# A two-pass Strassen FFN kernel: the second half of W is prepared inside the steps of the first pass, kept in DRAM, and loaded back slice by slice

## The chip, the cores and the metric

The kernel runs on one core of one Trainium2 chip. The metric is device time in microseconds from one launch to its end, less is better. The core has a matrix engine (TensorE, PE in the profile), a vector engine (VectorE, DVE), a scalar engine (ScalarE, ACT), GpSimd (POOL), a queue engine that here only issues DMAs (SyncE, SP) and 16 DMA engines. The on-chip memories are SBUF (128 partitions) and PSUM (8 banks of 128 x 512 float32).

## The reference

```python
x = x + _L0_ffn_ref(_L0_cond_ref(x, itok_B_0_30, L0_cond_weights), W_base, b_base, W_gate, A, B)
# _L0_cond_ref: x [32,128,2048], w = weights[subjects] [32,128,128]
return jnp.einsum('bct,bcd->bdt', x, w)
# _L0_ffn_ref: OUT = DIM = 2048, E = 8 experts of rank R = 16, TOP_K = 2
result = jnp.einsum('bnd,od->bno', x, W_base) + b_base
logits = jnp.einsum('bnd,ed->bne', x, W_gate)
probs = softmax(logits); top_p, top_i = top_k(probs, 2); top_p = top_p / sum(top_p)
route_w = sum(one_hot(top_i, E) * top_p[..., None])
hw = jnp.einsum('bnd,erd->bner', x, A) * route_w[..., None]
return result + jnp.einsum('bner,eor->bno', hw, B) * SCALING
```

So each of 32 blocks of 128 tokens is multiplied by a small matrix of its own, and the result (128 x 2048) by W (2048 x 2048), with a bias, a routed low-rank term and the input added.

## The kernel before

**Tiling.** The contraction is cut in two: the first pass (steps n = 0 to 15) works with columns 0 to 1023 of W, the second (steps 16 to 31) with columns 1024 to 2047. A step takes two of the 32 blocks. The product of the block pair with half of W is done by a Strassen-Winograd scheme: seven products (`NPROD = 7`) of sub-blocks, each for two halves `s` of the outputs, so 14 products a step. Every operand is split into an upper and a lower float16 part, and a product is 4 chunks x 3 matmuls of 128 x 512 (`three`, L1121 to L1123). The first pass writes its sums to DRAM (`part_scratch`), the second loads them, adds its own and stores to the output.

**What W has to become.** `TT` holds the seven prepared right-hand operands (B11, B22, B21 and four sums T1 to T4), upper and lower parts, for both `s`. There is room in SBUF for one half of W. It is prepared by units `g` (eight to a half): load rows (`load_rows`), sum of magnitudes per row (`sum_rows`, L582, ACT), powers of two as scales (`w_scales`, DVE), turn on PE with a scaled diagonal (`w_quad`, L1150) and spread of the inverse scale (`spread`, L1132), upper parts on ACT (`upper`, L603 and L610), sums and lower parts on DVE (`w_sums_and_lower`), last lower parts on POOL (`w_lower`, L450). Units 0 to 7 are done at the start, around step 0. Units 8 to 15 are done between steps 15 and 16, when nothing reads `TT` any more: at the end of step 15 PE waits for the last tiles and then turns all eight (L1367 to L1374), and before step 16 it waits for all of `w_lo`, `w_sum_lo` and `w_inv` (L1341 to L1344).

**One step of the loop.** No scheduler is at work: each engine runs its own list in the order in which it is written, with semaphores between them. PE: product q0 of s = 0, `make_features` (bank_h, 48 matmuls of 136 columns), `transpose_maxima` (L1207), products q1 and q2, `spread_maxima` (L1211), then the other products with four `cond` groups for step n+1 (bank_c) between them. `cond(n+1, U_A11)` stands after product q5 of s = 0 and waits for `xp_lo`, the lower parts of the scaled x. The chain to it is: product q2, DVE `finish(n, 0, C11)` (L823, L827), DVE `scale_x` (L782 to L786), ACT `split_x_hi` (L529, L530), DVE `split_x_lo` (L791, L793). POOL adds the bias (L456) and the step's results (L475) to the 128 x 512 tiles of `x_res`. ACT copies finished banks (`copy_p`, L571; `copy_a`, L537) and makes upper parts of the left operands (`s_upper`, L556). SP stores and loads tiles (`store_tile`, `load_tile`), x and the small weights (`load_x`). The buffer `x_parts` (XP) holds the split x of the next step from `split_x_hi` until the last `cond` of the step.

## Time and profile before

| | us |
|---|---|
| median of 3 runs | 1634.38 (1634.27 to 1634.62) |
| the profiled execution | 1634.34 |
| its span, first to last instruction | 1632.6 |
| PE busy | 1536.8 (94%) |
| DVE busy | 1300.2 (80%) |
| ACT busy | 596.5 (37%) |
| POOL busy | 631.9 (39%) |
| DMA, mean | 124 GB/s, 39.8% of 16 engines |

The profiled execution is within 0.04 us of the median, and lies 1.7 us above its own span. The table is an average over two passes and two stretches of preparation. The page's 40 slices and a table by stretch tell these apart. Since one line of code serves many instructions, groups are read by tile: bank_x, bank_y and bank_z are products, bank_h features, bank_c `cond` and the maxima, bank_d the second pass's deltas.

### The profile page before, as it was taken

Reading aid. Unit: us, or ns where it says so; the run is one execution under the profiler, and the core shown is the slowest. Engines: PE = TensorE matmul, PEld = TensorE weight load, DVE = VectorE, ACT = ScalarE, POOL = GpSimd, SP = SyncE. Lnnn points to the kernel's source line nnn. Section 1 sums busy time; section 2 is a strip of 40 time slices with the busy share of each in tenths; the row PEclk is TensorE's granted clock in tenths of the full one; section 3 lists DMA queues with packets and bytes.
Section 4 is the critical chain, followed back from the end, with each engine's and each line's share of the span. In section 5 each row is a group of like instructions: output and inputs, shape, how many; then the busy total and the mean of one; then the engine's idle time right before and its main releaser. Section 6 shows DMA issues by size and latency. Waiting matters only on the chain.

```text
span 1632.6 us, 25730 instructions
## 1 busy us (share of the span) xinstructions
PE 1536.8 (94%) x9539; PEld 837.8 (51%) x9539; DVE 1300.2 (80%) x2228; ACT 596.5 (37%) x996; POOL 631.9 (39%) x473
## 2 busy tenths in 40 slices
PE   5667999999999999999668999999999999999998
PEld 5444555555555555555464555555555555555553
DVE  6666888888888888888776888888888888888874
ACT  6654333333333333333583323333322333332231
POOL 2534455555555555555453122222212221221222
PEclk8788999999999999999889999999999999999999
DMA  5332444444444444444731344343334434333432
GB/s 198 130 117 82 128 136 136 135 135 134 128 136 136 136 127 133 132 134 125 235 104 39 98 137 136 110 122 121 102 91 136 136 113 121 122 105 88 134 107 71
DMA packets 102911, 201.87 MB, mean 124 GB/s; under 512 B 10874, under 2 KB 24186, under 8 KB 102266
## 3 DMA queue, kind: packets, MB, share of 16 engines
q1 hardware_dynamic: 102786, 200.22, 39.8%
q8 instruction: 76, 1.25, 0.3%
q14 instruction: 49, 0.40, 0.1%
HBM read 128.96 MB, written 71.22 MB: 123 GB/s over the span
## 4 chain that ended last, share of the span: by engine, by line
PE 89%; DVE 5%; ACT 2%; issue 2%; DMA 1%; POOL 1%; POOLq 0%; SPq 0%; DVEq 0%; ACTq 0%
PE bank_x L1121 10%; PE bank_x L1122 10%; PE bank_x L1123 10%; PE bank_y L1123 10%; PE bank_y L1122 10%; PE bank_y L1121 10%; PE bank_z L1121 3%; PE bank_z L1123 3%; PE bank_z L1122 3%; PE bank_h L1122 3%; PE bank_h L1121 3%; PE bank_h L1123 3%; PE bank_c L1121 2%; PE bank_c L1123 2%; PE bank_c L1122 2%
## 5 line engine op out<-in xcount | busy, mean ns | idle before, releaser
L475 POOL TENSOR_TENSOR x_res<-x_res,t_sums 128x512 f32<-128x512 f32 x256 | 350.7, 1372 | 895.6 <-DVE t_sums L827 735.5
L1121 PE MATMUL bank_x<-TT,s_parts 128*128 128x512 f16 x768 | 295.5, 385 | 14.8 <-POOL TT L450 7.5
L1122 PE MATMUL bank_x<-TT,s_parts 128*128 128x512 f16 x768 | 295.0, 384 | 0.0
L1123 PE MATMUL bank_x<-TT,s_parts 128*128 128x512 f16 x768 | 294.6, 384 | 0.0
L1121 PE MATMUL bank_y<-TT,s_parts 128*128 128x512 f16 x768 | 291.2, 379 | 0.0
L1122 PE MATMUL bank_y<-TT,s_parts 128*128 128x512 f16 x768 | 291.1, 379 | 0.0
L1123 PE MATMUL bank_y<-TT,s_parts 128*128 128x512 f16 x768 | 291.1, 379 | 0.0
L571 ACT ACTIVATE p_copies<-bank_x,y_inv 128x512 f32<-128x512 f32 x128 | 87.8, 686 | 492.8 <-PE bank_x L1123 398.7
L827 DVE TENSOR_TENSOR t_sums<-t_sums,inv_w 128x512 f32<-128x512 f32 x256 | 218.6, 854 | 8.8
L800 DVE TENSOR_TENSOR s_parts<-a_full,s_parts 128x512 f16<-128x512 f32 x224 | 208.1, 951 | 7.5 <-ACT s_parts L556 7.5
L456 POOL TENSOR_TENSOR x_res<-x_res,BT 128x512 f32<-128x512 f32 x128 | 197.8, 1545 | 4.8 <-DMA x_res<-in_x_dram 3.3
L556 ACT ACTIVATE s_parts<-a_full 128x512 f16<-128x512 f32 x224 | 137.2, 627 | 117.3 <-DVE a_full L805 49.5
L823 DVE SCALAR_TENSOR_TENSOR t_sums<-bank_y,y_inv,p_copies 128x512 f32<-128x512 f32 x128 | 95.5, 746 | 103.1 <-PE bank_y L1123 102.3
L1121 PEld LDWEIGHTS bank_x<-TT,s_parts 128*128 128x128 f16 x768 | 75.8, 99 | 100.6 <-issue 19.0
L823 DVE SCALAR_TENSOR_TENSOR t_sums<-bank_x,y_inv,p_copies 128x512 f32<-128x512 f32 x128 | 95.4, 745 | 38.3 <-PE bank_x L1123 38.3
L1123 PEld LDWEIGHTS bank_x<-TT,s_parts 128*128 128x128 f16 x768 | 76.0, 99 | 93.3 <-issue 4.6
L1123 PEld LDWEIGHTS bank_y<-TT,s_parts 128*128 128x128 f16 x768 | 75.2, 98 | 90.7 <-issue 0.2
L537 ACT ACTIVATE a_full<-bank_c 128x512 f32<-128x512 f32 x128 | 76.2, 595 | 122.1 <-PE bank_c L1123 122.1
L1122 PEld LDWEIGHTS bank_x<-TT,s_parts 128*128 128x128 f16 x768 | 76.0, 99 | 84.8 <-issue 3.3
L1122 PEld LDWEIGHTS bank_y<-TT,s_parts 128*128 128x128 f16 x768 | 75.2, 98 | 81.7 <-issue 0.3
L1121 PEld LDWEIGHTS bank_y<-TT,s_parts 128*128 128x128 f16 x768 | 75.2, 98 | 81.2 <-issue 0.3
L1121 PE MATMUL bank_c<-w_cond_parts,x_parts 128*128 128x128 f16 x512 | 93.7, 221 | 3.7 <-ACT a_full L537 3.7
(219 smaller groups left out, 2715.6 us busy)
## 6 DMA issues: line engine op xcount, KB each, us to landing
x<-in_x_dram SPq DMA_DIRECT2D x32, 1024.0 KB, 5.7
x_res<-in_x_dram SPq DMA_DIRECT2D x128, 256.0 KB, 3.7
part_scratch<-x_res SPq DMA_DIRECT2D x128, 256.0 KB, 2.9
x_res<-part_scratch SPq DMA_DIRECT2D x128, 256.0 KB, 3.9
out_dram<-x_res SPq DMA_DIRECT2D x128, 256.0 KB, 2.8
x_parts<-in_L_ffn_W_base_dram SPq DMA_DIRECT2D x12, 512.0 KB, 5.3
a_full<-in_L_ffn_W_base_dram SPq DMA_DIRECT2D x12, 512.0 KB, 4.8
w_cond<-in_L_cond_weights_dram SPq DMA_DIRECT2D x64, 64.0 KB, 3.9
```

The lines of the kernel that those rows point to most:

```text
L456: link(nc.gpsimd.tensor_tensor(XR[:, xr_slot(m), :], XR[:, xr_slot(m), :], bias[:, o:o + Q], ALU.add))
L475: nc.gpsimd.tensor_tensor(XR[:, xr_slot(m), :], XR[:, xr_slot(m), :], TM[:, m % 2, :], ALU.add).then_inc(r_added, 1)
L537: nc.scalar.activation(AF[:, u, :], BC[:, :], ACT.Copy, scale=Y_DOWN).then_inc(af_copied, 1)
L556: nc.scalar.activation(SO[:, slot(n, q), 0, :, :], quads(AF[:, af_of[q], :]), ACT.Copy).then_inc(s_hi, 1)
L571: nc.scalar.activation(PC[:, at, :], src[:, :], ACT.Copy, scale=y_inv[:, par, row:row + 1]).then_inc(p_copied, 1)
L800: nc.vector.tensor_tensor(SO[:, slot(n, q), 1, :, :], quads(AF[:, af_of[q], :]), SO[:, slot(n, q), 0, :, :], ALU.subtract).then_inc(s_lo, 1)
L823: nc.vector.scalar_tensor_tensor(out=TM[:, m % 2, :], in0=src[:, :], scalar=y_inv[:, n % 2, c // 2:c // 2 + 1], in1=PC[:, at, :], op0=ALU. ...
L827: nc.vector.tensor_tensor(TM[:, m % 2, :], TM[:, m % 2, :], inv_w[:, o:o + Q], ALU.mult).then_inc(r_ready, 1)
L1121: nc.tensor.matmul(dst, lhs[0], rhs[0], start=start, stop=False, skip_group_check=chained)
L1122: nc.tensor.matmul(dst, lhs[0], rhs[1], start=False, stop=False, skip_group_check=chained)
L1123: return nc.tensor.matmul(dst, lhs[1], rhs[0], start=False, stop=stop, skip_group_check=chained)
```

## The change

The preparation of units 8 to 15 moves into steps 1 to 15 of the first pass, under new numbers g = 0 to 7. A unit is cut into four chunks of 128 columns. `WINDOWS` gives each step two chunks, and step 7 all four of unit 3, so that 15 steps do 32 chunks.

- SP loads the unit's rows into `x_parts` once the last `cond` of the step has read it (`load_rows_ahead`), again for the second window.
- At the end of the step before a unit's first window ACT sums the rows (`sum_rows_ahead`), DVE makes scales (`scales_ahead`), PE spreads them into bank_d (`spread_ahead`); ACT scales the rows in place in front of every window (`scale_rows_ahead`).
- A chunk is turned by four float32 transposes into bank_d (`turn_chunk`), copied by ACT into a half of `a_full` (`copy_chunk`), added up to the four sums by four 128 x 128 operations on POOL (`add_up`), split into an upper part of 128 x 896 by ACT (`upper_chunk`) and a lower part of 128 x 896 by DVE (`lower_chunk`).
- SP stores each part to DRAM (`store_piece`, 896 pieces of 256 bytes, 64 stores). Three buffers take turns; they lie in `late_words`, a region shared with names that the first preparation and the second pass use.
- In step 15 ACT issues 14 loads of 1 MB, one for each q and s, as soon as that slice's last product is done (`load_weights`), and each product of step 16 waits for its own slice (`t_in`). `inv_w` goes through DRAM too. The loads of `FT`, `h_first` and `BT` for the second pass come earlier.
- `SLOTS` goes from 10 to 9, and `copy_p(n, 1, U2_COPY)` comes ahead of the upper part of S3. The whole block between steps 15 and 16 is gone.

The diff, cut to its core, in the order names, SP, POOL, ACT, DVE, PE:

```diff
-SLOTS = 10
+SLOTS = 9
...
+        NPIECE = 3
+        pieces = late_words[:, 0:1344].bitcast(F16).rearrange("p (i q n) -> p i q n", i=NPIECE, q=NPROD)
...
+        WINDOWS = []
+        for g in range(NU):
+            WINDOWS += [(g, (0, 1, 2, 3))] if g == WHOLE else [(g, (0, 1)), (g, (2, 3))]
+        SAVED = (B11, B22, B21, T1, T3, T2, T4)
...
+            def load_rows_ahead(g, chunks):
+                s, r = g // 4, g % 4
+                for i in range(2):
+                    o = s * KH + i * Q + r * P
+                    if chunks[0] == 0:
+                        sp.dma_start(xp_rows[:, i, :], w_base[o:o + P, KH:T]).then_inc(bg_rows[i], 16)
...
+            def store_piece(g, c, part):
+                s, r = g // 4, g % 4
+                sp.wait_ge((bg_hi, bg_lo)[part], n_chunk(g, c))
+                at = piece(g, c, part)
+                sp.dma_start(wt_dram[:, s, :, part, c, r * P:(r + 1) * P].rearrange("q p n -> p q n"), pieces[:, at, :, :]
+                             ).then_inc(bg_out[at], 16)
...
+                g, chunks = window_of(n)
+                if chunks:
+                    if chunks[0] == 0:
+                        store_inv(g)
+                    store_piece(g, chunks[0], 0)
+                    store_piece(g, chunks[0], 1)
+                    store_piece(g, chunks[1], 0)
...
                     store_tile(m)
+                    if len(chunks) == 2 and j == 0:
+                        store_piece(g, chunks[1], 1)
...
-                    if n == NP - 1 and j == 3:
+                    if n < len(WINDOWS) and j == (4 if n == 0 else 3):
+                        sp.wait_ge(cond_done, 4 * (n + 2))
+                        load_rows_ahead(*window_ahead(n))
...
-                    for g in range(NU + 2, 2 * NU):
-                        sp.wait_ge(w_tr, 4 * (g - 1))
-                        load_rows(g)
+                    load_inv(1)
...
+            def add_up(g, c):
+                chunk = full[c % 2].rearrange("p (i n) -> p i n", i=8)
+                pool.wait_ge(bg_copied, n_chunk(g, c))
+                nc.gpsimd.tensor_tensor(chunk[:, 5, :], chunk[:, 2, :], chunk[:, 0, :], ALU.subtract)
+                link(nc.gpsimd.tensor_tensor(chunk[:, 4, :], chunk[:, 0, :], chunk[:, 1, :], ALU.subtract))
+                link(nc.gpsimd.tensor_tensor(chunk[:, 6, :], chunk[:, 2, :], chunk[:, 4, :], ALU.subtract))
...
+                    g, chunks = window_of(n - 1)
+                    if chunks:
+                        act.wait_ge(bg_tr, n_chunk(g, chunks[-1]))
...
+                if chunks and u in (0, 2):
+                    act.wait_ge(bg_lo, n_chunk(g, chunks[-2 + u // 2]))
...
+            def sum_rows_ahead(g):
...
+                for i in range(2):
+                    act.wait_ge(bg_rows[i], 16 * n_window(g, 0))
+                    ins = nc.scalar.activation(late_words[:, 0:KH].bitcast(F16)[:, i * KH:(i + 1) * KH],
+                                               xp_rows[:, i, :], ACT.Abs, accum_out=row_sum[:, 0, i:i + 1])
+                ins.then_inc(bg_sums, 1)
+            def scale_rows_ahead(g, chunks):
+                act.wait_ge(bg_scaled, g + 1)
+                for i in range(2):
+                    act.wait_ge(bg_rows[i], 16 * n_window(g, chunks[0]))
+                    rows = halves(xp_rows[:, i, :], chunks)
+                    ins = nc.scalar.activation(rows, rows, ACT.Copy, scale=row_scale[:, i:i + 1])
+                ins.then_inc(bg_rows_scaled, 1)
...
+            def copy_inv_ahead(g):
+                act.wait_ge(bg_spread, g + 1)
+                if g > 0:
+                    act.wait_ge(bg_inv_out, 16 * g)
+                nc.scalar.copy(inv_piece, BD[:, 0:2 * P]).then_inc(bg_inv, 1)
+            def copy_chunk(g, c):
+                act.wait_ge(bg_tr, n_chunk(g, c))
+                if g == WHOLE and c >= 2:
+                    act.wait_ge(bg_lo, n_chunk(g, c - 2))
+                else:
+                    act.wait_ge(s_lo, NPROD * (n_window(g, c) + 1))
+                nc.scalar.activation(full[c % 2][:, 0:Q], BD[:, :], ACT.Copy).then_inc(bg_copied, 1)
+            def upper_chunk(g, c):
+                act.wait_ge(bg_sum, n_chunk(g, c))
+                at = piece(g, c, 0)
+                if piece_turn(g, c, 0) > 16:
+                    act.wait_ge(bg_out[at], piece_turn(g, c, 0) - 16)
+                nc.scalar.activation(pieces[:, at, :, :], full[c % 2][:, P:8 * P].rearrange("p (q n) -> p q n", q=NPROD),
+                                     ACT.Copy).then_inc(bg_hi, 1)
+            def load_weights(s, q):
+                act.wait_ge(prod_done, n_prod(NP - 1, s, q))
...
+                act.dma_start(TT[:, q, s, :, :, :], wt_dram[SAVED.index(q), s, :, :, :, :]).then_inc(t_in[s][q], 16)
...
+                if chunks and chunks[0] == 0:
+                    copy_inv_ahead(g)
...
+                if chunks:
+                    copy_chunk(g, chunks[0])
+                    copy_chunk(g, chunks[1])
+                    upper_chunk(g, chunks[0])
                 copy_p(n, 0, P5_COPY)
+                if chunks:
+                    upper_chunk(g, chunks[1])
+                if whole:
+                    copy_chunk(g, chunks[2])
                 copy_p(n, 0, U2_COPY)
...
+                if fresh:
+                    for q in range(4):
+                        load_weights(0, q)
...
                     lift_s(n + 1, U_A22, A22)
                     s_upper(n + 1, S4)
+                    copy_p(n, 1, U2_COPY)
                     s_upper(n + 1, S3)
-                    copy_p(n, 1, U2_COPY)
+                    if fresh:
+                        for q in range(5):
+                            load_weights(1, q)
...
+                g, chunks = window_ahead(n)
+                if chunks and chunks[0] == 0:
+                    sum_rows_ahead(g)
+                elif chunks:
+                    scale_rows_ahead(g, chunks)
                 copy_p(n, 1, P4_COPY)
-                if n == NP - 1:
-                    sum_rows(NU)
-                    for g in range(NU, 2 * NU):
-                        if g + 1 < 2 * NU:
-                            sum_rows(g + 1)
-                        w_upper(g)
-                    act.wait_ge(w_sum_lo, 4 * 2 * NU)
+                if chunks and chunks[0] == 0:
+                    scale_rows_ahead(g, chunks)
...
+            def scales_ahead(g):
+                dve.wait_ge(bg_sums, g + 1)
+                power_of_two(row_pow2[:, :], row_sum[:, 0, :], row_clamped[:, :])
+                link(nc.vector.reciprocal(row_rpow2[:, :], row_pow2[:, :]))
+                if g > 0:
+                    dve.wait_ge(bg_rows_scaled, n_window(g, 0) - 1)
+                    dve.wait_ge(bg_spread, g)
+                nc.vector.tensor_scalar(row_scale[:, :], row_rpow2[:, :], TOP_W, None, ALU.mult).then_inc(bg_scaled, 1)
...
+                ins.then_inc(bg_diag, 1)
+            def lower_chunk(g, c):
+                dve.wait_ge(bg_hi, n_chunk(g, c))
+                if n_chunk(g, c) > 1:
+                    dve.wait_ge(bg_lo, n_chunk(g, c) - 1)
+                at = piece(g, c, 1)
+                if piece_turn(g, c, 1) > 16:
+                    dve.wait_ge(bg_out[at], piece_turn(g, c, 1) - 16)
+                nc.vector.tensor_tensor(pieces[:, at, :, :], full[c % 2][:, P:8 * P].rearrange("p (q n) -> p q n", q=NPROD),
+                                        pieces[:, piece(g, c, 0), :, :], ALU.subtract).then_inc(bg_lo, 1)
...
+                if chunks:
+                    lower_chunk(g, chunks[0])
...
                     scale_x(n + 1)
+                if chunks and not whole:
+                    lower_chunk(g, chunks[1])
...
+                if ahead_chunks and ahead_chunks[0] == 0:
+                    scales_ahead(ahead)
...
-                if n == NP - 1:
-                    dve.wait_ge(r_added, 8 * NP)
-                    w_scales(NU)
-                    for g in range(NU, 2 * NU):
-                        if g + 1 < 2 * NU:
-                            w_scales(g + 1)
-                        w_sums_and_lower(g)
...
+                if n == NP:
+                    pe.wait_ge(t_in[s][q], 16)
...
+            def spread_ahead(g):
+                pe.wait_ge(bg_diag, g + 1)
...
+                mm.then_inc(bg_spread, 1)
+            def turn_chunk(g, c):
+                pe.wait_ge(bg_rows_scaled, n_window(g, c))
+                if c == 0:
+                    pe.wait_ge(bg_inv, g + 1)
+                else:
+                    pe.wait_ge(bg_copied, n_chunk(g, c - 1))
+                for i, (block_of, half) in enumerate(((1, 0), (0, 0), (1, 1), (0, 1))):
+                    mm = nc.tensor.transpose(BD[:, i * P:(i + 1) * P],
+                                             xp_rows[:, block_of, half * Q + c * P:half * Q + (c + 1) * P], ident[:, :])
+                mm.then_inc(bg_tr, 1)
...
                 product(n, 0, 0)
+                if chunks:
+                    turn_chunk(g, chunks[0])
                 make_features(n)
                 if more:
                     transpose_maxima(n + 1)
+                if chunks:
+                    turn_chunk(g, chunks[1])
...
-                if n == NP - 1:
-                    pe.wait_ge(p_copied, n_copy(n, 1, P4_COPY))
-                    pe.wait_ge(t_done, n_tile(n, 1, C22))
-                    pe.wait_ge(h_ready, NP)
-                    for g in range(NU, 2 * NU):
-                        pe.wait_ge(stage_in[2 * g % 4], 16 * (g // 2 + 1))
-                        pe.wait_ge(stage_in[(2 * g + 1) % 4], 16 * (g // 2 + 1))
-                        w_quads(g)
+                if ahead_chunks and ahead_chunks[0] == 0:
+                    spread_ahead(ahead)
```

**Order on PE**, in a step of the first pass, at the end of the features (bank_h) and the start of product q1 (bank_y). Before:

```order
2278 L1122 MATMUL bank_h<-FT,s_parts 128x136
2279 L1123 MATMUL bank_h<-FT,s_parts 128x136
2280 L1121 MATMUL bank_h<-FT,s_parts 128x136
2281 L1122 MATMUL bank_h<-FT,s_parts 128x136
2282 L1123 MATMUL bank_h<-FT,s_parts 128x136
2283 L1207 MATMUL bank_c<-ident,amax 4x128
2284 L1121 MATMUL bank_y<-TT,s_parts 128x512
```

After, in the step that begins a unit; here the spread, the end of product q0 with the first turn, and the second turn:

```order
2243 L1471 MATMUL bank_d<-diag_inv,ones 128x128 x2
...
2254 L1358 MATMUL bank_x<-TT,s_parts 128x512
2255 L1359 MATMUL bank_x<-TT,s_parts 128x512
2256 L1481 MATMUL bank_d<-ident,x_parts 128x128 x4
2257 L1357 MATMUL bank_h<-FT,s_parts 128x136
...
2305 L1445 MATMUL bank_c<-ident,amax 4x128
2306 L1481 MATMUL bank_d<-ident,x_parts 128x128 x4
2307 L1357 MATMUL bank_y<-TT,s_parts 128x512
```

Two groups of four float32 transposes stand between product q0 and product q1 of every such step, and a spread in front of q0 where a unit begins.

**Order on DVE**, from the top pair found (`find_top`, L777) to the lower part of x (L791). Before:

```order
280 L777 TENSOR_SCALAR top_diag<-ident,top_pow 4x4
281 L823 SCALAR_TENSOR_TENSOR t_sums<-bank_y,y_inv,p_copies 128x512
282 L827 TENSOR_TENSOR t_sums<-t_sums,inv_w 128x512
283 L782 COPY pow<-bank_c 128x4
284 L783 RECIPROCAL rpow<-pow 128x4
285 L784 TENSOR_SCALAR xw_scale<-rpow 128x4
286 L785 TENSOR_TENSOR x<-x 128x512
287 L786 SCALAR_TENSOR_TENSOR y_inv<-pow 128x2
288 L791 SCALAR_TENSOR_TENSOR x_parts<-x,xw_scale,x_parts 128x1024
```

After:

```order
294 L980 TENSOR_SCALAR top_diag<-ident,top_pow 4x4
295 L1185 TENSOR_TENSOR late_words<-a_full,late_words 128x896
296 L1028 SCALAR_TENSOR_TENSOR t_sums<-bank_y,y_inv,p_copies 128x512
297 L1032 TENSOR_TENSOR t_sums<-t_sums,inv_w 128x512
298 L985 COPY pow<-bank_c 128x4
299 L986 RECIPROCAL rpow<-pow 128x4
300 L987 TENSOR_SCALAR xw_scale<-rpow 128x4
301 L988 TENSOR_TENSOR x<-x 128x512
302 L989 SCALAR_TENSOR_TENSOR y_inv<-pow 128x2
303 L1185 TENSOR_TENSOR late_words<-a_full,late_words 128x896
304 L994 SCALAR_TENSOR_TENSOR x_parts<-x,xw_scale,x_parts 128x1024
```

One lower part stands in front of C11's finish, the other between `scale_x` and `split_x_lo`.

**Order on ACT**, from the end of one step's second half to the upper part of x in the next. Before:

```order
149 L556 ACTIVATE s_parts<-a_full 128x512 x3
150 L571 ACTIVATE p_copies<-bank_x,y_inv 128x512
151 L571 ACTIVATE p_copies<-bank_z,y_inv 128x512
152 L571 ACTIVATE p_copies<-bank_x,y_inv 128x512
153 L571 ACTIVATE p_copies<-bank_y,y_inv 128x512
154 L571 ACTIVATE p_copies<-bank_x,y_inv 128x512
155 L529 ACTIVATE x_parts<-x,xw_scale 128x1024
```

After, where a unit begins:

```order
166 L678 ACTIVATE s_parts<-a_full 128x512
167 L741 ACTIVATE late_words,row_sum<-x_parts 128x1024 x2
168 L693 ACTIVATE p_copies<-bank_z,y_inv 128x512
169 L750 ACTIVATE x_parts<-x_parts,row_scale 128x2x256 x2
170 L757 CAST late_words<-bank_d 128x256
171 L693 ACTIVATE p_copies<-bank_x,y_inv 128x512
172 L765 ACTIVATE a_full<-bank_d 128x512 x2
173 L772 ACTIVATE late_words<-a_full 128x896
174 L693 ACTIVATE p_copies<-bank_y,y_inv 128x512
175 L772 ACTIVATE late_words<-a_full 128x896
176 L693 ACTIVATE p_copies<-bank_x,y_inv 128x512
177 L648 ACTIVATE x_parts<-x,xw_scale 128x1024
```

Nine instructions are woven between the copies that PE and DVE wait for.

## Rows read from the trace of the kernel before

**Rows 1.** The page, 40 slices of the span: PE busy, in tenths.

```profile
PE   5667999999999999999668999999999999999998
```

**Rows 2.** By stretch: us, PE, PEld, DVE, ACT, POOL busy; clock; DMA share; GB/s.

```profile
180.00:780.00 600.00, 600.00 (x3803) 314.78 (x3801) 483.95 (x611) 205.67 (x329) 333.97 (x230) 1.00 0.43 134
780.00:860.00 80.00, 50.57 (x329) 42.54 (x327) 56.56 (x124) 56.47 (x108) 40.87 (x35) 0.85 0.50 162
```

**Rows 3.** Instructions of L1211 (behind product q2), by windows: count, ns, first and last start.

```profile
L1211 PE MATMUL bank_c<-top_diag,ones x1: 173/173/173, 171.4 to 171.4; 4*128 4x4 bf16 x1
...
L1211 PE MATMUL bank_c<-top_diag,ones x1: 172/172/172, 760.8 to 760.8; 4*128 4x4 bf16 x1
...
L1211 PE MATMUL bank_c<-top_diag,ones x1: 173/173/173, 878.5 to 878.5; 4*128 4x4 bf16 x1
```

**Rows 4.** Timeline of PE between steps 15 and 16: start, us, instruction, idle before, releaser.

```profile
800.79 0.37 PE L1132 MATMUL bank_h<-diag_inv,ones 128*128 128x128 bf16 x2 [8.57 <-DVE diag_inv L927]
...
865.68 0.59 PE L1121 MATMUL bank_x<-TT,s_parts 128*128 128x512 f16 x1 [7.45 <-POOL TT L450]
```

**Rows 5.** Timeline of PE: four float32 transposes early on; one, and a product, mid-pass.

```profile
25.09 0.60 PE L1266 MATMUL bank_d<-ident,TT 128*128 128x128 f32 x4
...
460.69 0.27 PE L1207 MATMUL bank_c<-ident,amax 128*4 128x128 f32 x1
460.80 0.38 PE L1121 MATMUL bank_y<-TT,s_parts 128*128 128x512 f16 x1
```

**Rows 6.** Timeline of a step of the first pass: the chain to `cond(n+1, U_A11)`.

```profile
426.92 1.79 POOL L456 TENSOR_TENSOR x_res<-x_res,BT 128x512 f32<-128x512 f32 x1
...
428.99 1.29 DVE L791 SCALAR_TENSOR_TENSOR x_parts<-x,xw_scale,x_parts 128x1024 f16<-128x1024 f32 x1 [0.26 <-ACT w_cond_parts L530]
...
430.20 0.35 DVE L793 SCALAR_TENSOR_TENSOR w_cond_parts<-w_cond,xw_scale,w_cond_parts 128x128 f16<-128x128 f32 x1
...
431.86 0.22 PE L1121 MATMUL bank_c<-w_cond_parts,x_parts 128*128 128x128 f16 x1
...
432.53 0.38 PE L1121 MATMUL bank_x<-TT,s_parts 128*128 128x512 f16 x1
```

**Rows 7.** Timeline of DVE: a lower part of 512 columns, beside POOL's work and without.

```profile
438.67 1.75 DVE L800 TENSOR_TENSOR s_parts<-a_full,s_parts 128x512 f16<-128x512 f32 x1
...
446.49 0.68 DVE L800 TENSOR_TENSOR s_parts<-a_full,s_parts 128x512 f16<-128x512 f32 x1
```

**Rows 8.** Timeline of DVE: the longest idle time of a step of the first pass.

```profile
466.18 0.75 DVE L823 SCALAR_TENSOR_TENSOR t_sums<-bank_y,y_inv,p_copies 128x512 f32<-128x512 f32 x1 [3.87 <-PE bank_y L1123]
```

**Rows 9.** One line's instructions: the sum of a row block on ACT (ns min/median/max).

```profile
L582 ACT ACTIVATE TT<-a_full x12: 1039/1056/1057, 80.0 to 843.5; 128x1024 f16<-128x1024 f32 x12
L582 ACT ACTIVATION_READ_ACCUMULATOR TT<-a_full x12: 185/186/187, 81.0 to 844.5; 128x1 f32 x12
```

**Rows 10.** Timeline of PE: q4 behind step 0's last `cond`; step 1's features.

```profile
152.78 0.38 PE L1121 MATMUL bank_z<-TT,s_parts 128*128 128x512 f16 x1
...
163.15 0.22 PE L1121 MATMUL bank_h<-FT,s_parts 128*128 128x136 f16 x1
```

**Rows 11.** DMA issues: KB each, median us from issue to landing.

```profile
x_parts<-in_L_ffn_W_base_dram SPq DMA_DIRECT2D x12, 512.0 KB, 5.3
...
h_scratch<-h SPq DMA_DIRECT2D x16, 136.0 KB, 2.3
...
BT<-bt_scratch SPq DMA_DIRECT2D x1, 1024.0 KB, 7.6
```

**Rows 12.** DMA from 434 to 435 us, then 435 to 436: packets by size; busy share.

```profile
DMA packets 96, 0.39 MB, mean 393 GB/s; under 512 B 0, under 2 KB 0, under 8 KB 96
...
q1 hardware_dynamic: 96, 0.39, 95.7%
...
DMA packets 328, 0.31 MB, mean 314 GB/s; under 512 B 39, under 2 KB 260, under 8 KB 328
...
q1 hardware_dynamic: 328, 0.31, 101.3%
```

167 lines of the change are left out of this document (134 added, 33 removed).

## The prediction

> **What bounds the kernel now.** I read the page's slices first, then the table by stretch, then the marks of the steps, then the timelines. The slices show PE at nine tenths or more, with holes at the start and near the middle [rows 1]. By stretch: from 180 to 780 us PE is busy 600.00 of 600.00 us at clock 1.00, DVE 81%, POOL 56%, ACT 34%, the DMA engines 43% [rows 2]. So in the first pass the step's length is PE's own work, and what any other engine does there costs nothing as long as it doesn't keep PE waiting. From 780 to 860 us PE is busy 50.6 of 80 us [rows 2].
>
> The length of a step: L1211 stands once in a step, behind product q2. Its marks at 171.4 (step 1) and 760.8 (step 15) are 14 steps apart [rows 3], so a step takes 589.4 / 14 = 42.1 us. From step 15's mark to step 16's (878.5) there are 117.7 us. Between the two lie the same products, features and `cond` groups as between any two marks of the first pass. So the preparation in the middle costs 117.7 - 42.1 = **75.6 us**. It contains 8.57 us of waiting for the first diagonals and 7.45 us for POOL's last lower parts, and step 16's first matmul takes 0.59 us [rows 4] against 0.38 elsewhere [rows 5], at a mean clock of 0.85 in that stretch [rows 2]: part of the 75.6 us is the lower of the clock's two levels after waiting.
>
> **What the change removes.** Nothing stands between step 15 and step 16 any more, and PE doesn't go idle, so it has no reason to come back at the lower clock. If the slices of `TT` are there in time, the whole 75.6 us go. What then is late next is what the rest of the sum is about.
>
> **PE's new work.** 32 chunks of four float32 transposes. Such a transpose leaves 0.11 us until the next matmul mid-pass (460.69 to 460.80), and four take 0.60 us to the last one's end, 0.27 us of which overlaps what follows [rows 5]. That makes 0.44 us a chunk, at most 0.60: 14.1 us, at most 19.2. The eight spreads are two short matmuls each, at most 0.22 us; I take 0.15, so 1.2 us. All of it lies on the path, since PE is the bound: **+15.3 us** (up to 21). A step becomes 43.1 us.
>
> **The chain to `cond(n+1, U_A11)`** is where the new work comes nearest to PE. Before, DVE ends the first half's lower parts at 430.20 + 0.35 = 430.55, and PE starts the `cond` at 431.86 [rows 6]: 1.31 us of slack. All its links hang on product q2, which the turns shift as much as the `cond`, so the slack stays. But a `lower_chunk` now stands between `scale_x` and `split_x_lo`. 512 columns of the same kind take 0.68 us [rows 7], 1024 take 1.29 [rows 6], so 896 take 1.14. DVE had 0.26 us to wait there anyway [rows 6], so the chain gets 0.88 us longer and 0.43 us of slack remain. If POOL is in the middle of a tile then, a DVE operation with two SBUF inputs waits: the same lower part takes 1.75 us instead of 0.68 [rows 7]. That adds 1.07 us and makes a stall of 0.64. POOL gets eight more operations of 128 columns a step. None is in the trace; by a 512-column operation such as the 1.79 us one [rows 6] they lie between a quarter of it and all of it. I take 0.45 us each, since no row shows a large fixed part, so 3.6 us on top of POOL's 23.4. It meets DVE more often. I take 0.5 us a step on average over 15 steps, between 0 and 2: **+7.5 us** (0 to 30).
>
> The other additions have cover. The first `lower_chunk` stands where DVE waits 3.87 us for bank_y [rows 8]. ACT gets two copies of 512 columns, two upper parts of 896 and two scalings of 512 a step, some 4 us by 1.06 us for 1024 columns [rows 9], on an engine that is two thirds idle [rows 2]. `SLOTS` at 9 makes each upper part wait for one product later, which is done when its turn comes; only S3's now waits for the end of q4, and the U2 copy was put ahead of it.
>
> **Starts of units.** DVE must wait for the sum of the rows: two times 1.06 + 0.19 us on ACT [rows 9], against one or two lower parts of 0.68 us of its own, so some 1.6 us; six small operations for scales and diagonals I put at 1.2 us. Everything behind on DVE (`find_maxima`, C12, C21, C22) is 2.8 us later eight times, and POOL's results with it. The idle 3.87 us in front of C11 [rows 8] takes that up; what it doesn't is within the 0.5 us a step. At the end of step 0 it isn't covered: the last `cond` ends at 152.78 [rows 10], the rows need 5.3 us [rows 11] and 0.5 for a second issue, the sum 2.5, the scales 1.2: 162.3 us. Step 1's features start at 163.15 [rows 10], one product behind q6, which so ends at 160.56. PE stands 1.7 us before the spread: **+1.7 us**. Step 7 has four chunks, where copies, sums and `split_x_hi` queue behind one another: **+1.5 us**, by the chain above once more or twice.
>
> **The stores.** 64 stores of 896 pieces of 256 bytes. In one microsecond 96 packets of 4 KB keep the engines 96% busy: 0.16 us of an engine for each. In the next one 328 packets, 260 of them small (mostly 512 bytes), fill it too [rows 12]: 16 us less about 8 for the 68 large ones, over 260, is 0.03 us each. By that a store takes 57 packets an engine x 0.03 = 1.8 us and about 2 us of latency (136 KB land in 2.3 us [rows 11]). The second lower part needs the buffer of the first upper part. That one is made by about 9 us into the step (product q0, a turn, a copy, POOL's tile and sums, the 896 columns) and stored at some 9.5; the second lower part starts at about 16.5 (three products, the features, C11 and `scale_x`). So 3 us remain. The engines get 4 x 1.8 us a step on top of 18, and some 2 for the rows of W: two thirds busy. Ends: 0.03 us as for 512 bytes, and 0.16 us as for a 4 KB packet, since nothing in the trace forbids it for so short a write. I take the near one: no cost.
>
> The Trainium skill speaks against such stores: DMA: Bandwidth & Descriptors, section Specifications, says that transfers under 512 bytes are done as read-modify-write. No run here shows a write that small. If that doubled the 0.03 us, a store would land in 5.5 us instead of 3.8, still within the 7, and the sum would be the same.
>
> **The slices of `TT`.** 14 loads of 1 MB. A product is 2.59 us (step 0's q4 to q6 and step 1's q0 take 163.15 - 152.78 = 10.37 us [rows 10]), a `cond` 432.53 - 431.86 = 0.67 [rows 6]. The first load is issued behind q4's copy in step 15, nine products and four `cond` before step 16: 26 us. The last is needed 13 products and some 11 us of features, `cond` and deltas into it: 45 us. At 393 GB/s [rows 12] they take 37 us of all engines; the regular traffic takes 0.43 of 71 us [rows 2], and FT and BT 5: 72 of 71 us. That just fits, and each product needs only its own slice. I take **+2 us** (0 to 35).
>
> **Sum.** 1634.3 - 75.6 + 15.3 + 7.5 + 1.7 + 1.5 + 2.0 = **1587 us**. The median of before is the profiled execution's own time within 0.04 us, so nothing is to be scaled.
>
> **Rivals.**
> - *Forecast*, 1578 to 1599: chance 0.50.
> - *No stalls*: the lower part always falls between POOL's operations, and loads and stores stay hidden. 1634.3 - 75.6 + 14 to 19 us of PE's work = 1573 to 1578. For it: the 0.43 us left. Against: step 0's wait has no cover. 0.13.
> - *The woven chain is longer than I see*: a chunk passes PE, ACT, POOL, ACT, DVE, and the tile work behind each is pushed in turn, so PE waits 1.5 to 2.5 us in each of 15 steps: 1600 to 1620. For it: POOL's and DVE's blocking of each other, and DVE at 81% before [rows 2]. 0.22.
> - *The slices come late*: 1 MB from DRAM took 7.6 us once [rows 11]. At that pace, one after another, 14 take 106 us, the last is there some 35 us late: 1585 + 35 = 1620. Against: other transfers ran beside that one. 0.07.
> - *Slower than before, by small stores*: if a packet of 256 bytes holds an engine x us, a step keeps the engines 20 + 4 x 57x us. They become the bound above 43.1 us, x = 0.10, and the gain is gone when a step takes 43.1 + 60.3 / 15 = 47.1 us, x = 0.12. At 0.16 the step is 56.5 us, the kernel 1634.3 - 60.3 + 15 x 13.4 = 1775. The 512-byte packets say 0.03. 0.06.
> - The rest, 0.02, ends about where the kernel is now.
>
> 0.2% (3.3 us) is about what a measurement of this kernel can tell from no change. Faster 0.92, same 0.02, slower 0.06. The range goes from the case without stalls to most of the longer chain: 1573 to 1614.
>
> **What would show it.** The marks behind q2 stand 43.1 to 43.7 us apart from step 1 to 15 and from step 16 on as before, and 43 us from step 15 to 16; no idle time over 1 us of PE but at step 0's end; PE at clock 1.00 across the middle. DVE's 128 x 896 operation near 1.14 us, near 2.2 where POOL is busy. A store of pieces lands in about 4 us. Wrong would be: PE idle before `cond` in every step (the chain), before q1 (a turn waits for ACT's copy), or at step 16's products with the DMA engines full (the slices); and a DMA share near 1 in the first pass (the stores).

## The result, and the profile after

The changed kernel takes **1621.57 us** (median of 4 runs, 1619.79 to 1623.09) against 1634.33 for the one before (4 runs): ratio **0.9923**, 95% interval 0.9905 to 0.994. The forecast was 1587 us, range 1573 to 1614. It is 0.8% faster, clear of noise, but by 13 us and not by 47, and the time lies above the range.

The profiled execution took 1619.79 us. Its page, 40 slices (answers [rows 1]), and the spans by stretch (answer [rows 2]; columns as there):

```profile
span 1618.0 us, 25812 instructions
...
PE   5667999999989999999989999999999999999997
...
DMA  5333555555555555555598334434333443333442
```

```profile
173.50:808.70 635.20, 611.55 (x3859) 323.44 (x3858) 542.47 (x675) 279.43 (x446) 414.81 (x349) 0.99 0.55 163
```

```profile
808.70:860.70 52.00, 43.80 (x267) 23.28 (x266) 37.46 (x48) 15.47 (x25) 21.45 (x16) 0.93 0.96 375
860.70:910.90 50.20, 47.96 (x293) 24.50 (x292) 42.32 (x95) 15.14 (x26) 11.80 (x9) 1.00 0.64 197
```

The hole in the middle of [rows 1] is gone: where 117.7 us lay between the marks of steps 15 and 16 [rows 3], there are 52.0. But PE is no longer busy all the time in the first pass. It waits 23.7 us of the 635.2 between the marks of steps 1 and 15, and in the first of the two stretches behind the DMA engines come to 0.96 of their time (0.64 in the second). The marks behind product q2 of steps 1, 15, 16 and 17 (they answer [rows 3]):

```profile
L1449 PE MATMUL bank_c<-top_diag,ones x1: 173/173/173, 173.5 to 173.5; 4*128 4x4 bf16 x1
```

```profile
L1449 PE MATMUL bank_c<-top_diag,ones x1: 173/173/173, 808.7 to 808.7; 4*128 4x4 bf16 x1
```

```profile
L1449 PE MATMUL bank_c<-top_diag,ones x1: 173/173/173, 860.7 to 860.7; 4*128 4x4 bf16 x1
```

```profile
L1449 PE MATMUL bank_c<-top_diag,ones x1: 173/173/173, 910.9 to 910.9; 4*128 4x4 bf16 x1
```

By the sum, step 15's mark stands at 760.8 + 15.3 + 7.5 + 1.7 + 1.5 = 786.8 us; it stands at 808.7, **21.9 us** later. From there to step 17's mark the sum has 42.1 + 47.5 + 2.0 = 91.6 us; it took 102.2, **10.6 us** more. These two places are 32.5 us; the profiled execution misses the forecast by 32.8.

What PE waited for from 173 to 920 us (us in total, times, longest):

```profile
PE bank_c L1357 <- DVE w_cond_parts L996: 16.4, 14, 3.0
PE bank_h L1357 <- issue: 8.0, 1, 8.0
PE bank_d L1481 <- ACT a_full L765: 3.3, 1, 3.3
```

The first line is `cond(n+1, U_A11)`, about once in a step: the chain of [rows 6]. The second is step 16's features, which need `FT`: its load landed at 851 us, when they began. The third is a turn in step 7, the step of the whole unit. No product waited for a slice of `TT`. The chain in step 3, in order of time (timeline: start, us, instruction, idle before, releaser), with POOL's four sums of the second chunk (L565 to L568) at its head:

```profile
261.86 1.31 POOL L565 TENSOR_TENSOR a_full<-a_full 128x128 f32<-128x128 f32 x1
263.13 0.45 POOL L566 TENSOR_TENSOR a_full<-a_full 128x128 f32<-128x128 f32 x1
263.66 0.89 POOL L567 TENSOR_TENSOR a_full<-a_full 128x128 f32<-128x128 f32 x1
264.63 1.00 POOL L568 TENSOR_TENSOR a_full<-a_full 128x128 f32<-128x128 f32 x1
```

```profile
265.67 0.95 ACT L772 ACTIVATE late_words<-a_full 128x896 f16<-128x896 f32 x1 [3.44 <-POOL a_full L568]
...
267.10 1.14 ACT L648 ACTIVATE x_parts<-x,xw_scale 128x1024 f16<-128x1024 f32 x1
```

```profile
268.56 1.58 DVE L994 SCALAR_TENSOR_TENSOR x_parts<-x,xw_scale,x_parts 128x1024 f16<-128x1024 f32 x1 [0.63 <-ACT w_cond_parts L649]
...
269.14 2.13 POOL L587 TENSOR_TENSOR x_res<-x_res,t_sums 128x512 f32<-128x512 f32 x1
...
270.07 1.35 DVE L996 SCALAR_TENSOR_TENSOR w_cond_parts<-w_cond,xw_scale,w_cond_parts 128x128 f16<-128x128 f32 x1
```

```profile
271.47 0.23 PE L1357 MATMUL bank_c<-w_cond_parts,x_parts 128*128 128x128 f16 x1 [1.01 <-DVE w_cond_parts L996]
```

`split_x_hi` (L648) starts 4.7 us behind the step's mark (262.4), since ACT stands 3.44 us in front of the second upper part (L772) until POOL has made its sums. And the last two links on DVE (L994, L996) take 1.58 and 1.35 us beside POOL's tile, where [rows 6] has 1.29 and 0.35. In [rows 6] the step's mark is at 171.4 + 6 x 42.1 = 424.0 us; DVE starts the first of the two 4.99 us behind it and ends the second 6.55 us behind it, here 6.15 and 9.01. Of these 2.46 us more, 1.16 come from ACT's queue and 1.29 from DVE's two operations. The slack of 1.31 us takes up about half, and PE waits for the rest, 1.01 us. In step 2 ACT is free in time (`split_x_hi` starts 3.7 us behind the mark), and it is DVE's operations that are long beside POOL: the second lower part takes 2.13 us instead of 1.09, and C11's finish (L1032) 1.61 instead of 0.69:

```profile
221.83 1.67 POOL L587 TENSOR_TENSOR x_res<-x_res,t_sums 128x512 f32<-128x512 f32 x1
223.47 1.27 POOL L559 TENSOR_TENSOR x_res<-x_res,BT 128x512 f32<-128x512 f32 x1
```

```profile
219.01 1.61 DVE L1032 TENSOR_TENSOR t_sums<-t_sums,inv_w 128x512 f32<-128x512 f32 x1
...
223.56 2.13 DVE L1185 TENSOR_TENSOR late_words<-a_full,late_words 128x896 f16<-128x896 f32 x1
```

### The profile page after: what moved, and what is told of

The parts are those of the page before. It is cut to its first block, busy times and chain, and to the rows that moved or that the text cites. A ratio compares the mean times of both kernels' runs of the same rounds, so it can differ in the third digit from the quotient of the medians.

```text
span 1618.0 us, 25812 instructions
## 1 busy us (share of the span) xinstructions
PE 1518.1 (94%) x9411; PEld 814.1 (50%) x9411; DVE 1311.6 (81%) x2196; ACT 626.3 (39%) x1026; POOL 686.6 (42%) x569
## 4 chain that ended last, share of the span: by engine, by line
PE 61%; DVE 18%; issue 7%; POOL 7%; DMA 4%; ACT 3%; SPq 1%; POOLq 0%; ACTq 0%; DVEq 0%
PE bank_x L1357 7%; PE bank_x L1358 7%; PE bank_x L1359 7%; PE bank_y L1359 6%; PE bank_y L1357 6%; PE bank_y L1358 6%; DVE s_parts L1003 3%; POOL x_res L587 3%; DVE t_sums L1028 2%; PE bank_h L1358 2%; PE bank_h L1359 2%; PE bank_h L1357 2%; PE bank_z L1357 2%; PE bank_z L1359 2%; PE bank_z L1358 2%
## 5 line engine op out<-in xcount | busy, mean ns | idle before, releaser
L587 POOL TENSOR_TENSOR x_res<-x_res,t_sums 128x512 f32<-128x512 f32 x256 | 360.5, 1408 | 827.0 <-DVE t_sums L1032 665.2
L1032 DVE TENSOR_TENSOR t_sums<-t_sums,inv_w 128x512 f32<-128x512 f32 x256 | 231.7, 905 | 8.8
L1003 DVE TENSOR_TENSOR s_parts<-a_full,s_parts 128x512 f16<-128x512 f32 x224 | 199.5, 907 | 38.2 <-ACT s_parts L678 38.2
L559 POOL TENSOR_TENSOR x_res<-x_res,BT 128x512 f32<-128x512 f32 x128 | 201.1, 1571 | 28.7 <-DMA x_res<-in_x_dram 27.2
L1357 PE MATMUL bank_c<-w_cond_parts,x_parts 128*128 128x128 f16 x512 | 93.5, 221 | 20.4 <-DVE w_cond_parts L996 16.4
```

The costliest lines, as they stand in the source:

```text
L559: link(nc.gpsimd.tensor_tensor(XR[:, xr_slot(m), :], XR[:, xr_slot(m), :], bias[:, o:o + Q], ALU.add))
L587: nc.gpsimd.tensor_tensor(XR[:, xr_slot(m), :], XR[:, xr_slot(m), :], TM[:, m % 2, :], ALU.add).then_inc(r_added, 1)
L1003: nc.vector.tensor_tensor(SO[:, slot(n, q), 1, :, :], quads(AF[:, af_of[q], :]), SO[:, slot(n, q), 0, :, :], ALU.subtract).then_inc(s_lo, 1)
L1032: nc.vector.tensor_tensor(TM[:, m % 2, :], TM[:, m % 2, :], inv_w[:, o:o + Q], ALU.mult).then_inc(r_ready, 1)
L1357: nc.tensor.matmul(dst, lhs[0], rhs[0], start=start, stop=False, skip_group_check=chained)
```

## The experiments

Each row has the stretch from step 1's mark to step 15's and the one from there to step 17's, in one profiled execution, and the median of 4 to 11 timed ones. The same code repeats less well than before: the first stretch, with all of the change in it, was 635.2, 633.4, 633.0 and 638.2 us in the four kernels that don't touch it (the changed one, e3, e5, e4). So nothing is read from 5 us there. e4, e8, e9, e15 and e18 leave out a part of the work or store it elsewhere, and their output isn't the reference's: they price something and are no better kernels.

| kernel | 1 to 15 | 15 to 17 | median us | ratio |
|---|---|---|---|---|
| before | 589.4 | 165.2 | 1633 to 1634 | 1 |
| changed | 635.2 | 102.2 | 1621.6 | 0.9923 |
| e1 DVE's second lower part late | 631.5 | 104.2 | 1622.4 | 0.9934 |
| e2 also ACT's second upper part | 627.6 | 106.7 | 1619.7 | 0.9917 |
| e3 FT ahead of the slices | 633.4 | 106.6 | 1623.9 | 0.9937 |
| e4 no slices loaded | 638.2 | 90.2 | 1609.2 | 0.9851 |
| e5 last seven slices in step 16 | 633.0 | 100.6 | 1614.1 | 0.9886 |
| e6 = e2 + e5 | 627.5 | 96.3 | 1607.3 | 0.9852 |
| e7 = e6 + spread later | 624.5 | 95.6 | 1605.2 | 0.9836 |
| e8 wide stores | 629.4 | 105.2 | 1618.6 | 0.9919 |
| e9 one sum on POOL for four | 612.1 | 107.0 | 1602.7 | 0.9806 |
| e10 = e6 + fourth turn later | 629.5 | 97.2 | 1610.8 | 0.9867 |
| e11 = e7 + e10 | 625.5 | 97.5 | 1607.0 | 0.9837 |
| e12 = e11 + e3 | 624.8 | 95.4 | 1604.9 | 0.9822 |
| e13 sums on DVE | 640.4 | 103.0 | 1627.9 | 0.9973 |
| e14 = e13 + e5 + e3 | 640.4 | 95.4 | 1619.9 | 0.9912 |
| e15 = e9 + e5 + e3 | 610.6 | 93.5 | 1589.7 | 0.973 |
| e16 sums in three, + e5 + e3 | 630.5 | 97.0 | 1610.6 | 0.9853 |
| e17 = e16 + e7's edits | 628.6 | 94.8 | 1608.9 | 0.985 |
| e18 sums of 32 columns, + e5 + e3 | 617.2 | 96.5 | 1597.7 | 0.978 |

### Which queue makes the wait: e1 and e2

e1 moves a line on DVE. e2 also moves ACT's `upper_chunk(g, chunks[1])` behind both `split_x_hi`, and SP's store of the second chunk's upper part behind its first tile store, where that of the lower part stands already. e1's edit:

```diff
-                if chunks and not whole:
-                    lower_chunk(g, chunks[1])
                 if more:
                     split_x_lo(n + 1, 0)
                     split_x_lo(n + 1, 1)
+                if chunks and not whole:
+                    lower_chunk(g, chunks[1])
```

> The only edit is on VectorE: in the steps with two chunks, the second lower part (1.1 us) goes behind both split_x_lo, so that it no longer lies on the way from x to the conditioning transform. The changed kernel is at 1621.6 us, and TensorE waits there about 1.1 us in each of some 13 steps (16.4 us in 14 waits). Theory A (ScalarE's queue): what is late is split_x_hi, because upper_chunk stands ahead of it on ScalarE and waits for GpSimd's add_up; VectorE's lower part lies in the shadow of that. Then the waits stay at 0.6 to 1.1 us each, and the time is 1612 to 1622. Theory B (VectorE's queue, the term of my prediction): the 1.1 us of the lower part is the whole of the wait. Then the waits vanish in the regular steps, steps last 43.1 to 43.3 us in place of 44.2, and the time is about 1606.

> As in the run before, and on ScalarE too the second upper_chunk goes behind both split_x_hi; SyncE's stores of the second chunk move behind its first tile store, since their data come later. Theory A (ScalarE's queue and VectorE's lower part together make the wait): the waits for the conditioning transform vanish in the regular steps (43.1 to 43.3 us each in place of 44.2), and the long wait after step 14 with its clock fall goes too: 1600 to 1605 us. Theory B (VectorE alone): the same time as the run before within 1 us. Theory C (GpSimd's work lies on the path by its lock on VectorE, whatever the order of the queues): waits of 0.5 us or more stay in both runs, 1610 or more.

Neither theory held for e1. The wait vanished in the steps that finish a unit (2, 4, 6) and doubled in steps that begin one (3, 5, 10, 12), where the sums on POOL and ACT's upper part stand ahead:

```profile
271.48 0.23 PE L1357 MATMUL bank_c<-w_cond_parts,x_parts 128*128 128x128 f16 x1 [1.94 <-DVE w_cond_parts L996]
```

In e2 the waits fell to 0.3 to 0.75 us, but a second chain came up: the next unit's rows, sums and scales, for which PE now waits at the end of a step:

```profile
340.90 0.29 PE L1474 MATMUL bank_d<-diag_inv,ones 128*128 128x128 bf16 x2 [1.64 <-DVE diag_inv L1177]
```

Steps 1 to 15 lost 7.6 us (5.4 against the shortest of the four above), half of what the waits for `cond` had been. And nothing of it came through: step 17's mark stood at 910.7 us, where it had been at 910.9. The two steps behind had grown by 4.5.

### The two steps behind step 15: e3 to e6

e3 takes FT's load from SP to ACT; e4 takes the loads of the slices out:

```diff
                if fresh:
+                    act.wait_ge(h_done, NP)
+                    act.wait_ge(ft_out, 16)
+                    act.dma_start(FT[:, :, :, :].rearrange("p f s n -> p (f s n)"), ft_dram).then_inc(ft_in, 16)
                    for q in range(4):
                        load_weights(0, q)
```

```diff
-                act.dma_start(TT[:, q, s, :, :, :], wt_dram[SAVED.index(q), s, :, :, :, :]).then_inc(t_in[s][q], 16)
...
-                if n == NP:
-                    pe.wait_ge(t_in[s][q], 16)
```

> The load of the features FT is issued on ScalarE's queue ahead of the 14 slices of W's second half, instead of on SyncE's queue behind the loads and stores of the last step, where it was issued at 837 us and took 13.7 us. Theory A: the wait of 8.0 us ahead of step 16's features and the half clock after it (about 2 us) are the price of that late load; step 15 to 16 falls from 52.0 to 43 to 44 us, and the time by 8 to 10 us to about 1612. Theory B (the transfers are full, whatever the order: 0.96 of the engines' time in this stretch): then the slices, or the last step's own loads, are late instead, the two steps behind 808.7 us keep a sum of over 100 us, and the time is within 3 us of 1621.6.

> The 14 loads of W's second half and TensorE's waits for them are left out, so that the second pass computes with the first half's tiles; all the stores stay. What the loading back costs in all is the difference. Expected: step 15 to 16 about 43.1 us in place of 52.0 and step 16 to 17 47.5 in place of 50.2, together 11.6 us, 1610 us. If instead FT's late load has another cause than the slices (SyncE's own queue), the wait of about 8 us ahead of step 16 stays, and the time is 1618 to 1621.

e4 prices the reload: 102.2 - 90.2 = 12.0 us, in the median time 12.3. The DMA engines are full: from 808 to 861 us, issues with KB each and median us to landing,

```profile
TT<-wt_scratch ACTq DMA_DIRECT2D x14, 1024.0 KB, 12.1
...
x<-in_x_dram SPq DMA_DIRECT2D x1, 1024.0 KB, 20.8
FT<-ft_scratch SPq DMA_DIRECT2D x1, 816.0 KB, 13.7
...
h_scratch<-h SPq DMA_DIRECT2D x1, 136.0 KB, 20.9
```

The slices arrive in time; what is late is the short traffic of the ordinary step beside them. The store of `h` takes 20.9 us (2.3 in [rows 11]; 2.5 in e4), FT's load stands behind a load that waits for that store, and so is issued at 837.38 and lands at 851. In e3 FT landed in 6.0 us, and x's load was late instead (23.6 us for 20.8; DVE waited 5.33 us for it), so that the next step's scales were; BT's load was late, too:

```profile
857.08 0.18 PE L1449 MATMUL bank_c<-top_diag,ones 4*128 4x4 bf16 x1 [3.90 <-DVE top_diag L980]
...
878.14 0.59 PE L1357 MATMUL bank_d<-BT,late_words 128*128 128x512 f16 x1 [4.52 <-DMA BT<-bt_scratch]
```

e5 takes the loads (1, 0) to (1, 6) from the end of step 15 on ACT into step 16, behind `exps` and around the U2 copy:

```diff
+                if n == NP:
+                    for q in range(3):
+                        load_weights(1, q)
...
+                if n == NP:
+                    load_weights(1, 3)
+                    load_weights(1, 4)
                 copy_p(n, 0, U2_COPY)
+                if n == NP:
+                    load_weights(1, 5)
+                    load_weights(1, 6)
```

> The changed kernel, with one edit: the seven slices that belong to step 16's second half are issued on ScalarE inside step 16 (three behind its first copy, two ahead of and two behind its third), not at the end of step 15 where they were issued at 837 to 841 us. They are needed from about 878 us. Theory A (the 14 slices together fill the transfers from 815 to 862 us, and what is late are the short loads and stores between them: the store of h landed after 21 us, FT's load is issued behind it and takes 13.7 us): with the last seven gone from that stretch FT's load lands within 6 us and the wait of 8.0 us goes. Step 15 to 16 falls from 52.0 to 43 to 45 us and 16 to 17 stays at 47.5 to 50: 1610 to 1613 us. Theory B (the bytes are the bound, so an order only moves the wait, as FT ahead of the slices did: two steps together 106.6 us in place of 102.2): the two steps keep 100 us or more, and TensorE waits for the late slices in step 16: 1619 to 1624 us.

> The edit of e5_pace with that of e2_both_late (the second upper and lower chunk behind both halves of x's split). In e2_both_late steps 1 to 15 ended 4.7 us earlier than in the changed kernel (804.0 against 808.7 us), and the wait for FT grew by as much, so that nothing was left of it. Theory A (that gain was held up by the transfers alone): the gain comes through once they are paced, and this kernel is 4 to 6 us below e5_pace, 1604 to 1608 us. Theory B (the transfers bound this stretch by their bytes): e6_pace_both is equal to e5_pace within 1 us.

e5 gave 7.5 us by the medians; its profiled execution took 1618.7 us, the far side of a range of 1611.8 to 1620.1; in it PE waited 5.4 us for BT's load. The other executions weren't traced, so whether that makes the spread isn't shown. e6 is 6.8 us below e5 by the medians, as theory A said: e2's gain, which had vanished, comes through once the transfers are spaced out. Its own forecast was 4 to 6 us.

### The next chains: e7, e10, e11, e12

e7's edit on PE, where `later` is 1 in a step that begins a unit (but not in step 1), and the spread at a step's end is gone; then e10's:

```diff
-                if chunks:
+                if later:
+                    spread_ahead(g)
+                elif chunks:
                     turn_chunk(g, chunks[0])
                 make_features(n)
...
-                    turn_chunk(g, chunks[1])
+                    turn_chunk(g, chunks[1 - later])
```

```diff
-                    if len(chunks) > 2 and q < 3:
-                        turn_chunk(g, chunks[q + 1])
+                    if len(chunks) > 2 and q in (1, 3):
+                        turn_chunk(g, chunks[2 if q == 1 else 3])
```

> e6_pace_both, with TensorE's spread of the next unit's scales moved from a step's end to behind the next step's first product, and in those steps each turn moved one place back. In e2_both_late every second step lasted 43.3 us, but those between them 43.8 to 45.8, with TensorE waiting 1.0 to 1.6 us for the diagonal of scales (rows loaded when x's buffer is free, summed on ScalarE, scaled on VectorE). Theory A (this chain of the next unit's rows is the next limit, 1 us behind the conditioning chain): its waits vanish, the steps that begin a unit fall to about 43.3 us, and the time is 4 to 8 us below e6_pace_both, 1598 to 1603 us. Theory B (the chain is not short by the place of the spread; the copy of the inverse and the turn behind it are then late): the same wait appears at the turn, and the time is that of e6_pace_both within 2 us.

> e6_pace_both (1607.3 us) with one edit: in the whole unit's step the fourth chunk is turned on TensorE behind product 3 in place of product 2. In e6_pace_both TensorE waits 3.8 us there for ScalarE's copy of the third chunk (it stands behind two upper parts that wait for GpSimd), and then runs at half clock for some 4 us; steps 7 and 8 last 50.4 and 48.2 us together with 98.6 us against 87.0 for two regular ones. Theory A (the place of this turn makes some 5 us of it): TensorE's wait falls to about 1.2 us, the clock stays up, the two steps together last 93 to 95 us, and the time is 1602 to 1604 us. Theory B (the chain of four chunks through two buffers sets the end, whatever TensorE does meanwhile): x's split, which overwrites the rows, or the fourth chunk's parts are late instead, the conditioning transform waits 2 to 4 us longer, and the time stays at 1606 to 1609 us.

> All edits together: second chunk's parts behind x's split, slices paced, the spread of scales behind the next step's first product (as in e7_all, but for the whole unit as before), the whole unit's fourth turn later. If the edits add up (e7_all 1605.2 us, less what e10_whole_later gains): 1598 to 1602 us. If they share one limit (VectorE is busy for 0.90 of a step by then), no better than the best of them: 1603 to 1606 us.

> e11_combined with FT's load issued on ScalarE ahead of the first seven slices, instead of on SyncE behind the load of h that waits 18 to 21 us for h's store. In e7_all TensorE still waits 3.7 us for FT, followed by the half clock. Alone this edit gained nothing (106.6 us for the two steps). Theory A (with the last seven slices paced, the short transfers that were late then have room): the wait for FT goes and nothing takes its place, 3 to 5 us below e11_combined. Theory B (the first seven slices alone hold up x's load, which then makes the maxima and their spread late, as in e3_ft_first): the same time as e11_combined within 1 us, or slower.

e7's waits for the diagonals went, but its time fell by 2.2 us only: regular steps stayed at 43.4 to 44.2 us, with 0.2 to 0.7 us of waiting for `cond`, and from step 6's mark to step 9's there were 142.6 us, as in e6 (142.4). In e10 the turn waited 1.0 us in place of 3.8, and `cond` waited 3.2 us nine microseconds later (453.42). This is what theory B says, that the chain of four chunks through two buffers sets the end; the time, 1610.8 us, is even 3.5 us above e6's. e11 (1607.0) is no better than e7, which fits one limit shared by the moves, but no run shows which. e12 is 2.1 us below e11, between its two theories. e12 at 1604.9 us (0.9822, interval 0.9809 to 0.9835) and e7 are the fastest of those that compute everything.

### The stores: e8

```diff
-                sp.dma_start(wt_dram[:, s, :, part, c, r * P:(r + 1) * P].rearrange("q p n -> p q n"), pieces[:, at, :, :]
-                             ).then_inc(bg_out[at], 16)
+                row = (2 * (C4 * g + c) + part) * P
+                sp.dma_start(wt_dram.rearrange("q s p a c n -> (q s p a c n)").rearrange("(r n) -> r n", n=NPROD * P)[row:row + P, :],
+                             pieces[:, at, :, :].rearrange("p q n -> p (q n)")).then_inc(bg_out[at], 16)
```

> The changed kernel with each piece of 224 KB stored as 128 rows of 1792 bytes in place of 896 rows of 256 bytes, at another place of the scratch; the output isn't the reference's, since the slices loaded back are then in another order. Same bytes, same waits. Theory A (the short rows cost: SyncE's queue stands 1.1 to 4.5 us on the issue of two such stores, a piece lands after 3.6 us, and VectorE waits 1.5 to 4.2 us for a piece's buffer in five places, which is most of the 13.6 us by which steps 7 to 9 are long): the store lands within 2.5 us, VectorE's waits for buffers go, steps 7 to 9 lose 3 to 8 us, and the time is 1612 to 1618 us. Theory B (the short rows cost nothing on the path, the whole unit is long by its chain of turn, copy, sums and parts): steps 7 to 9 stay within 2 us of 146.2 us together, and the time within 2 us of 1621.6.

3 us by the medians, between both theories. From 218 to 700 us a piece lands in 3.1 us in place of 3.5 (medians), and the three long waits of DVE for a piece's buffer in steps 7 and 8 became 3.64, 3.39 and 2.26 us from 4.03, 4.18 and 2.73 (4.05, 4.37 and 2.34 in e3, with the same code there as the changed kernel). PE waited 2.67 us behind the last of them, for 3.00 in the changed kernel, but for 2.68 and 2.67 in e3 and e5, too, so that this isn't the rows' doing. In the changed kernel's trace a packet of 256 bytes took an engine a median of 18 ns, one of 512 bytes 27, where the prediction had 0.03 us for either. (The text's 1.1 to 4.5 us for the issue of two stores are rows of the timeline in which two are merged with the time between them; from 218 to 700 us no single one took over 0.94 us.) Read-modify-write below 512 bytes (the Trainium skill, DMA: Bandwidth & Descriptors, Specifications) can at most be those 0.4 us of a store here. Taking no cost for the short rows was nearly right.

### POOL's sums: e9, e13 to e18

```diff
-                nc.gpsimd.tensor_tensor(chunk[:, 5, :], chunk[:, 2, :], chunk[:, 0, :], ALU.subtract)
-                link(nc.gpsimd.tensor_tensor(chunk[:, 4, :], chunk[:, 0, :], chunk[:, 1, :], ALU.subtract))
-                link(nc.gpsimd.tensor_tensor(chunk[:, 6, :], chunk[:, 2, :], chunk[:, 4, :], ALU.subtract))
-                nc.gpsimd.tensor_tensor(chunk[:, 7, :], chunk[:, 6, :], chunk[:, 3, :], ALU.subtract).then_inc(bg_sum, 1)
+                nc.gpsimd.tensor_tensor(chunk[:, 7, :], chunk[:, 2, :], chunk[:, 3, :], ALU.subtract).then_inc(bg_sum, 1)
```

> The changed kernel with one subtraction of 128x128 per chunk on GpSimd in place of four, so that the T parts are not computed and the output isn't the reference's; everything else stands as it is. Steps alternate in the changed kernel: where a unit begins (218 to 262 us) GpSimd's sums run at 0.45 us each and ScalarE is free 1.9 us ahead of split_x_hi; where it is finished (262 to 307 us) the second chunk's sums end at 265.6 us, ScalarE's upper part stands behind them, and split_x_hi starts 1.2 us later. TensorE waits about 1.0 us in both. Theory A (GpSimd's four sums are on the path in the finishing steps, VectorE's lower part and its lock in the beginning ones): the wait goes in every second step, which fall to 43.2 to 43.6 us, the others stay near 44.2 us; with the whole unit's chain also shorter, 1610 to 1615 us. Theory B (VectorE's lower part makes the wait in all steps; GpSimd's sums cost nothing on the path): all stay at 44.2 to 44.3 us, 1619 to 1622 us.

More than theory A had (1602.7 us for 1610 to 1615): the wait went from all regular steps, which last 43.1 us, with ACT's and DVE's queues as they were. (The text takes the two kinds of steps for each other: the one at 218 us finishes a unit, the one at 262 begins one.) PE by stretch, clock and DMA share at the end:

```profile
529.20:787.70 258.50, 258.50 (x1651) 137.86 (x1650) 229.27 (x288) 118.85 (x189) 149.28 (x108) 1.00 0.57 168
```

In the step at 218 us POOL's tile work now comes before DVE's lower part and no longer meets it, and DVE's last two links are back at 1.28 and 0.35 us (medians of steps 1 to 15; the second takes up to 1.35 in the changed kernel and never over 0.35 here). That is the other half of what the sums did:

```profile
221.49 1.79 POOL L559 TENSOR_TENSOR x_res<-x_res,BT 128x512 f32<-128x512 f32 x1
```

```profile
223.33 1.09 DVE L1182 TENSOR_TENSOR late_words<-a_full,late_words 128x896 f16<-128x896 f32 x1
```

And again the two steps behind ate a part: step 15's mark 21.0 us earlier, step 17's 16.2; PE waited 15.3 us for FT.

> The changed kernel with the same four subtractions per chunk on VectorE in place of GpSimd: the first chunk's ahead of the features, the second's behind the maxima's scale; all is computed. With three of GpSimd's four left out (e9_pool_one) the regular steps fell from 44.2 to 43.1 us and steps 1 to 15 by 21.0 us. Theory A (what cost was the chain through GpSimd: its queue, where sums stand behind an add that waits for VectorE, and the stretching of its and VectorE's operations while both run): VectorE takes the 2 us per step in the 4 to 5 us that it is idle, steps fall to 43.1 to 43.3 us, steps 1 to 15 by 15 to 20 us; the slices then hold the next two steps up, as in e9_pool_one (59.5 and 47.5 us), and the time is 1602 to 1606 us. Theory B (the work itself costs, on whichever engine, since VectorE is already busy for 0.88 of a step): VectorE's own operations come later instead, steps stay at 44 us or more, 1615 to 1625 us.

> e13_sums_on_dve with the last seven slices issued inside step 16 and FT's load ahead of the first seven. All is computed. Theory A (two separate causes: GpSimd's sums in steps 1 to 15, the transfers in the two steps behind): TensorE passes step 15 to 16 in 43 to 46 us and 16 to 17 in 47.5 to 49, where e9_pool_one took 107.0 for both, and the time is 1588 to 1595 us. Theory B (the transfers' bytes bound the stretch once TensorE comes earlier): the two steps keep 98 us or more, 1597 to 1603 us.

In e13 `add_up` is called on DVE with `nc.vector` in place of `nc.gpsimd`, for the first chunk ahead of `features(n)` and for the second behind `find_top(n + 1)`. That is worse than on POOL, and beyond theory B; e14 missed both its ranges with it (1619.9 us), though the two steps behind step 15's mark took 95.4 us there for 103.0. One of the four sums (L1168), in the same step for the first chunk, while POOL adds tiles, and for the second, while POOL is idle:

```profile
213.82 1.31 POOL L578 TENSOR_TENSOR x_res<-x_res,t_sums 128x512 f32<-128x512 f32 x1
```

```profile
213.93 1.35 DVE L1168 TENSOR_TENSOR a_full<-a_full 128x128 f32<-128x128 f32 x1
...
219.35 0.27 DVE L1168 TENSOR_TENSOR a_full<-a_full 128x128 f32<-128x128 f32 x1
```

1.35 against 0.27 us for the same subtraction: two engines whose operations shut each other out. DVE is busy 215.93 of 224.70 us there, and PE waits for `top_diag`, too, about 1.7 us in every second step. So the work is not free elsewhere, and whether it is dear hangs on where POOL stands. The Trainium skill (SBUF — State Buffer, SBUF: two separate sides) has this as an exclusive lock, held for a whole instruction; these rows agree, since a DVE operation with two SBUF inputs that alone takes 0.27 us lasts 1.35 us beside one of POOL's of 1.31.

> e9_pool_one (one subtraction per chunk, output not the reference's) with the same two edits to the transfers. What GpSimd's three other subtractions and the transfers' order cost together is the difference to the changed kernel, 1621.6 us. Theory A: mark 16 stays at about 788 us, the two steps behind it last 91 to 95 us, 1586 to 1591 us, equal to e14 within 3 us if VectorE takes the sums for nothing. Theory B (bytes): as e9_pool_one, 1600 us or more.

e15 has three of the four sums out and the transfers spaced, and gives back 31.9 of the changed kernel's 34.6 us above the forecast: 1589.7 us, as theory A said. That step 15's mark stands at 787.4 us, where my sum had 786.8, is luck: the sum holds 7.5 us of waits that e15 doesn't have, and only 1.5 for the whole unit, whose steps lose 7.5 there.

```profile
L1449 PE MATMUL bank_c<-top_diag,ones x1: 173/173/173, 787.4 to 787.4; 4*128 4x4 bf16 x1
```

e16 has T3 and T2 in one operation; e18 has four operations as before, each with `0:32` in place of `:`.

```diff
+                link(nc.gpsimd.tensor_tensor(chunk[:, 4, :], chunk[:, 0, :], chunk[:, 1, :], ALU.subtract))
+                link(nc.gpsimd.tensor_tensor(chunk[:, 5:7, :], chunk[:, 2:3, :].to_broadcast([P, 2, P]), chunk[:, 0:5:4, :],
+                                             ALU.subtract))
```

> The changed kernel with the two edits to the transfers (as in e15_pool_one_paced_ft) and the same sums on GpSimd in three operations in place of four: T3 and T2 in one operation of 256 columns. All is computed. With one operation per chunk steps 1 to 15 ended at 787 to 788 us, with four at 808.7, so each left out was worth 7 us if they count alike. Theory A (what counts is the number of operations, since each waits for a link to the one before and for VectorE's lock): steps 1 to 15 end 5 to 7 us earlier than 808.7 and the time is 1602 to 1608 us. Theory B (what counts is their work, the same columns): steps 1 to 15 end within 2 us of 808.7, 1608 to 1613 us.

> All edits that leave the output the reference's: three operations on GpSimd, the second chunk's parts behind x's split, the spread behind the next step's first product, the slices paced and FT ahead of them. The nearest so far, e12_combined_ft, was 1604.9 us. If three operations relieve what is left of the waits: 1597 to 1602 us. If the parts behind x's split already hid what they cost: 1603 to 1606 us.

> As e16_three_ops, but with all four operations on GpSimd at 32 columns in place of 128, so that three quarters of each T part are not computed and the output isn't the reference's. GpSimd's time alone falls from 0.45 us for each to some 0.25. Theory A (the number of operations counts, each held by the lock and by a link): the regular steps stay at 43.8 us or more and steps 1 to 15 end above 800 us; 1603 us or more. Theory B (the work counts): steps of 43.1 to 43.4 us, steps 1 to 15 end near 790 us, as with one operation, and the time is 1589 to 1594 us.

What goes by the number of operations and what by their columns: in 177 us (218 to 395) POOL spends 5.3 us on the sums in e9, 11.8 in e18, 18.4 in e16 and 20.3 in the changed kernel, and the stretch from step 1 to 15 takes 612.1, 617.2, 630.5 and 635.2 us. It follows POOL's time in order, though not in proportion, and not the number: four narrow operations (e18) are 13 us better than three wide ones (e16). Nor is it the columns alone: e9 and e18 have 128 of them in a chunk both. e18, at 1597.7 us with steps of 43.1 and 43.8 in turn, lies between its two theories. e17 at 1608.9 missed both its ranges: three operations for four, put on top of e7's moves, brought nothing beyond e12 (1604.9), and why isn't shown. Rows of the changed kernel and of e9 (count; busy us, mean ns):

```profile
L565 POOL TENSOR_TENSOR a_full<-a_full 128x128 f32<-128x128 f32 x8 | 7.0, 877 | 0.0
L567 POOL TENSOR_TENSOR a_full<-a_full 128x128 f32<-128x128 f32 x9 | 5.0, 552 | 0.7
L568 POOL TENSOR_TENSOR a_full<-a_full 128x128 f32<-128x128 f32 x8 | 4.7, 592 | 0.6
L566 POOL TENSOR_TENSOR a_full<-a_full 128x128 f32<-128x128 f32 x8 | 3.6, 449 | 0.0
```

```profile
L565 POOL TENSOR_TENSOR a_full<-a_full 128x128 f32<-128x128 f32 x8 | 5.3, 665 | 0.0
```

## Why the prediction was wrong

**What held.** The sign, and the 75.6 us: nothing of the old middle is left. PE's new work at 0.44 us a chunk: with the waits out (e9, e15) a step is 43.1 us to the tenth. The end of step 0: step 1's mark stands 2.1 us later, where 1.7 and two turns were priced (in other kernels with the same code there, up to 5.6 us later: e3). The pieces: a lower part of 896 columns takes 1.09 us free and 2.13 beside POOL (1.14 and 2.2 were given), a narrow sum 0.45 us when it is alone (but POOL's sums took 20.3 us in four steps, 5.1 a step and not 3.6), a store of pieces lands in 3.5 us, and the short rows cost next to nothing.

**The step that failed first: "the chain to `cond`".** That new work on this chain makes PE wait was right, and the rival "the woven chain is longer than I see" named more of it, but the price of 7.5 us was not: outside the three steps around the whole unit, the eleven from mark to mark between steps 1 and 15 took 489.0 us, 14.9 more than eleven of 43.1, where 0.5 us each, 5.5, were priced. I gave POOL's sums 3.6 us a step as load on POOL, and to the chain only the chance that they shut DVE out, 0.5 us. They are links of it as well. I had put ACT's two upper parts under "the other additions have cover", because ACT is two thirds idle. An idle engine whose queue stands before a wait is no cover: in step 3 the upper part waits 3.4 us for POOL, and `split_x_hi` stands behind it. And they push POOL's tile work back onto DVE's lower part and its last two links. With three of four sums out, the eleven lose nothing any more, and steps 1 to 15 are 23.1 us (e9) and 24.6 us (e15) shorter. Part of this is the clock: behind the waits of 3.31, 3.00 and 2.25 us it was at half for 3.4 us each time, some 1.7 us of PE's work lost in each (an estimate, half of 3.4).

**The whole unit's step** is the larger miss of the two. 1.5 us were priced, with 1.5 more for the chain in these three steps. From step 6's mark to step 9's there are 146.2 us, 16.9 more than three of 43.1; with one sum (e9) 138.3, 9.0 more. So some 8 us are the sums' again. What is left I put down to the chain of four chunks through two buffers; e10 showed that it isn't the place of a turn, and no run took the four chunks apart.

**The slices: the overlap.** 2 us were priced and some 12 came: 102.2 us against 42.1 + 47.5 = 89.6, and 12.0 by e4. My count of the bytes, 72 of 71 us, said itself that the engines would be full, and they were (0.96 of their time from step 15's mark to step 16's). The conclusion was wrong: I asked whether each slice is there when its product comes, and they were. What a queue of 1 MB loads does to the 136 KB and 816 KB transfers beside it, on which PE's features hang, I had not asked, and [rows 11] had shown the times of such transfers only with the engines at about 0.4 of their time. So PE did go idle in the middle, for 8.0 us, and the clock fell there, which "PE doesn't go idle" had ruled out. The order counts: with e5's and e3's edits together the two steps take 93.5 to 97.0 us (e12 and e14 to e18), with FT ahead alone 106.6. Without slices they take 90.2, and no run with all of them went below 93.5.

**Why the two errors hid each other.** Where step 15's mark came earlier, the transfers held up what is behind it for longer: it was 2.5, 4.7, 6.0 and 21.0 us earlier in e1, e2, e8 and e9, and the two steps behind took 2.0, 4.5, 3.0 and 4.8 us more. Of e1's and e2's gain nearly nothing reached step 17's mark, of e9's 16.2 us. By its median alone, 1.9 us, e2 would have been called worthless; on top of e5 it brings 6.8 us (e6).

What stays open: how much of the 23 us is POOL's place in the chain and how much the shutting out. Step 3's rows give 1.2 and 1.3 us of one step; the runs without sums changed both, and e2, which moves the parts and keeps the sums, got 7.6 us. Nor was a version tried that puts DVE's sums into POOL's idle time.

## What to carry to other kernels

Work woven into a full pipeline must be followed engine by engine to the instruction behind it in each queue: a queue that waits covers nothing, however idle its engine is. Follow the one irregular step (here that of the whole unit) by itself. For bulk transfers ask what small transfers travel beside them, not only whether the bulk is in time, and space it out. When a fix shows no gain in the end time, compare marks on the way before dropping it: a later limit may be holding the gain.

## What the runs showed of the hardware

Not every wait of PE is followed by a lower clock (columns: us, PE, PEld, DVE, ACT, POOL busy; clock; DMA share; GB/s). After 1.01 us of waiting at 271 the clock stays at its upper level, and so it did after 1.60 us at 481. Behind the wait of 3.00 us that ended at 504.5 it was at half, 1.2 of 2.4 GHz, from 505.8 to 509.2, and so it was for 3.4 us behind those of 3.31 and 2.25 us (at 443 and 772). In the wait of 8.0 us it fell at 847, four microseconds before PE had work again, and rose at 854:

```profile
272.00:274.00 2.00, 2.00 (x15) 1.04 (x13) 2.00 (x3) 1.23 (x2) 0.54 (x1) 1.00 0.84 254
```

```profile
506.00:508.00 2.00, 2.00 (x7) 0.63 (x5) 1.26 (x2) 0.63 (x1) 0.56 (x1) 0.50 0.45 57
...
847.00:851.00 4.00, 0.00 (x0) 0.00 (x0) 1.29 (x2) 0.00 (x0) 0.00 (x0) 0.52 1.03 423
851.00:855.00 4.00, 3.85 (x43) 3.88 (x44) 0.00 (x0) 0.00 (x0) 0.00 (x0) 0.63 1.02 420
```

So a wait of 3 us cost more here than three of 1 us. And with the DMA engines full, issuing was in part itself slow on SyncE, so that everything behind it in the queue was issued late. In the changed kernel and in e2 (issue us; the first row is of two issues, 2.89 and 1.48 us, 0.34 to 0.37 in the steps before):

```profile
819.59 5.13 SPq L376 DMA_DIRECT2D w_cond<-in_L_cond_weights_dram  x2
...
824.76 3.09 SPq L418 DMA_DIRECT2D x_res<-in_x_dram  x1
```

```profile
815.66 13.58 SPq L496 DMA_DIRECT2D h_scratch<-h  x1
```

Not every issue in such a stretch is slow: at 837 us, with the engines as full, `FT`'s took 0.39 us. What decides it, no run shows.
